# Whitening kernel: every matmul moved into 64x64 tiles of the array, with centring on GpSimd and stores from SyncE

## The reference

```python
mean = x1.mean(-1, keepdims=True)
xc = x1 - mean
cov = xc @ xc.transpose(0, 2, 1) / M + EPS * jnp.eye(G, dtype=x.dtype)
decorr = isqrt_newton_schulz(cov, N_ITER)
y = weight1 @ decorr @ xc + bias1
```

## Time and profile before

| what | value |
|---|---|
| median of 3 runs | 510.39 us |
| the three runs | 490.27, 510.39, 511.94 us |
| span of the profiled execution | 506.6 us |
| median less the span | 3.8 us |
| instructions in the span | 17928 |
| read from and written to HBM | 75.51 MB and 75.50 MB |
| mean rate of the DMA engines | 300 GB/s |
| TensorE busy, by matmuls | 450.2 us |
| TensorE busy, by weight loads | 285.0 us |
| VectorE busy | 329.5 us |
| ScalarE busy | 342.5 us |
| GpSimd busy | 56.6 us |

### The profile page before, as it was taken

One profiled execution on the slowest core, in us unless ns is written; L12 is line 12 of the kernel. 1 busy time (PEld: TensorE's weight loads), 2 busy tenths in 40 slices (PEclk: granted clock), 3 DMA queues, 4 the chain that ended last, 5 costly groups with the idle time before them and its releaser, 6 DMA issues.

```text
span 506.6 us, 17928 instructions
## 1 busy us (share of the span) xinstructions
PE 450.2 (89%) x7872; PEld 285.0 (56%) x7872; DVE 329.5 (65%) x1043; ACT 342.5 (68%) x450; POOL 56.6 (11%) x108
## 2 busy tenths in 40 slices
PE   3678899999999999999999999999999999888800
PEld 3667766666566666666656666666666556423200
DVE  6886567777877787877777877777777765321000
ACT  5674478887777787877778878888787744433800
POOL 0000001111111111111110111111111111110410
PEclk9795579999999999999999999999999989855855
DMA  8999707999899999999999999999998545635890
GB/s 344 371 420 423 314 3 226 345 361 353 315 340 340 351 337 360 374 380 365 323 363 363 341 376 349 372 340 347 379 361 270 178 153 172 187 119 141 265 285 11
DMA packets 19774, 152.17 MB, mean 300 GB/s; under 512 B 3056, under 2 KB 3056, under 8 KB 3696
## 3 DMA queue, kind: packets, MB, share of 16 engines
q0 software_dynamic: 9952, 75.50, 41.8%
q1 hardware_dynamic: 9744, 75.52, 40.7%
HBM read 75.51 MB, written 75.50 MB: 298 GB/s over the span
## 4 chain that ended last, share of the span: by engine, by line
PE 85%; DMA 2%; ACT 2%; DVE 2%; issue 2%; POOL 1%; SPq 1%; DVEq 0%; POOLq 0%
PE cov_ps L591 32%; PE y_ps L606 32%; PE chain_ps L566 6%; PE chain_ps L562 5%; DMA b_col<-bias 2%; PE shift_ps L525 2%; PE chain_ps L572 2%; ACT image L310 1%; PE chain_ps L541 1%; POOL y L272 1%; PE chain_ps L551 1%; PE chain_ps L574 1%; PE chain_ps L560 1%; PE chain_ps L564 1%; PE chain_ps L558 1%
## 5 line engine op out<-in xcount | busy, mean ns | idle before, releaser
L319 ACT ACTIVATE image<-y_ps,y_bias 128x768 f32<-128x768 f32 x192 | 172.2, 899 | 103.4 <-PE y_ps L606 91.8
L403 DVE STREAM_TRANSPOSE transposed<-image 128x384 f32<-128x384 f32 x384 | 213.5, 571 | 13.0 <-issue 2.0
L591 PE MATMUL cov_ps<-transposed 128*64 128x65 f32 x4608 | 188.4, 235 | 9.6 <-DVE transposed L403 7.3
L606 PE MATMUL y_ps<-image,apply_w 64*64 64x384 f32 x1536 | 180.5, 542 | 1.4 <-ACT image L319 0.9
L591 PEld LDWEIGHTS cov_ps<-transposed 128*64 128x64 f32 x4608 | 161.6, 146 | 18.5 <-issue 11.6
L310 ACT ACTIVATE image<-image,shift 128x1152 f32<-128x1152 f32 x128 | 158.1, 1246 | 1.5 <-DMA image<-x 0.5
L562 PEld LDWEIGHTS chain_ps<-yz 32*32 32x32 f32 x576 | 20.9, 106 | 91.7 <-DVE yz L455 54.2
L270 POOL DMA_DIRECT2D y<-image x34 | 19.4, 570 | 425.9 <-ACT image L319 425.9
L455 DVE COPY yz<-chain_ps 64x64 f32<-64x64 f32 x144 | 29.6, 206 | 45.2 <-PE chain_ps L566 39.2
L606 PEld LDWEIGHTS y_ps<-image,apply_w 64*64 64x64 f32 x1536 | 42.4, 138 | 24.5 <-ACT image L319 9.0
L451 DVE SCALAR_TENSOR_TENSOR t_mat<-chain_ps,eye 64x32 f32<-64x32 f32 x144 | 25.0, 174 | 30.3 <-PE chain_ps L562 28.6
(11 more groups left out here) (61 smaller groups left out, 155.6 us busy)
## 6 DMA issues: line engine op xcount, KB each, us to landing
image<-x SPq DMA_DIRECT2D x63, 1152.0 KB, 10.1
y<-image POOLq DMA_DIRECT2D x31, 1152.0 KB, 9.8
y<-image POOLq DMA_DIRECT2D x62, 576.0 KB, 11.0
image<-x SPq DMA_DIRECT2D x2, 576.0 KB, 4.2
y<-image POOLq DMA_DIRECT2D x3, 384.0 KB, 11.6
y<-image POOLq DMA_DIRECT2D x6, 192.0 KB, 11.3
w_nat<-weight SPq DMA_DIRECT2D x4, 4.0 KB, 10.4
b_col<-bias SPq DMA_DIRECT2D x4, 0.1 KB, 10.7
```

The costliest lines, as they stand in the source:

```text
L319: nc.scalar.activation(xs[slot_of(c, i)][:, :, STRIP * q:STRIP * (q + 1)], y_ps[:, q % 2, :, 0:STRIP], ACT.Identity, bias=y_bias[:, c % 2, ...
L403: nc.vector.transpose(dst, xs[slot_of(c, i)][:, h, of_half:of_half + PIECE // 2]).then_inc(transposed, 1)
L591: ins = nc.tensor.matmul(cov_ps[rows, i, 0:GRAM], xt[q][:, t, 0:WIDE * G], xt[q][:, t, 0:GRAM], start=q == 0 and t < columns, stop=q == IM ...
L606: ins = nc.tensor.matmul(y_ps[out_rows, q % 2, h, 0:STRIP], apply_w[rows, c % 2, i].rearrange("p k g -> p (k g)"), xs[slot_of(c, i)][rows, ...
```

## The change

The kernel was written anew around slots; what it computes is the same.

- **Product on the diagonal.** Row group r multiplies into column group r for both halves, so half 1 is no longer exchanged. Again four matmuls of 384 columns for a slot, two in each of two quarters instead of one in each of four. They are issued as two for half 0 and two for half 1.
- **Covariance on the other two quarters.** A matmul has 64 rows instead of 128 (row group r into column group 1-r) and 66 moving columns. Twice as many are needed: 24 in a slot, 12 in each of the two quarters, issued in two lots of 12.
- **Chain in one 64x64 tile.** The two images of a pair stand in one block-diagonal matrix; a step is one matmul of 64 rows and 64 columns with 32 or 96 moving columns, in the upper left quarter, the one that also has half of the product. VectorE's `factor` and `yz` grow with it (64x64 and 64x96 elements). GATHER no longer uses TensorE: ScalarE copies four 32x33 blocks of an image's covariance, and VectorE adds and finishes them (six operations, one a small transpose). NORM has six operations on VectorE.
- **Waits.** In most steps VectorE goes on to the transpose without waiting for its chain operation to end.
- **Order.** In each half slot TensorE issues a chain step, two product matmuls, then 12 covariance matmuls. The product runs 25 slots behind the covariance (`LAG`), and transposes 4 slots ahead (`LEAD`).
- **Centring** is on GpSimd, in 192 operations of 768 pixels, instead of 128 of 1152 on ScalarE.
- **Stores** are issued by SyncE, two for each image, each with 128 partitions. The load into the slot of image n-1 is issued after the store of image n. The small weights are loaded from ScalarE's queue at the start.

The heart of the diff:

```diff
-                columns = BLOCKS // WIDE
-                places = TILES // WIDE
-                for t in range(places):
-                    rows = slice(WIDE * G * (t % columns), WIDE * G * (t % columns + 1))
-                    ins = nc.tensor.matmul(cov_ps[rows, i, 0:GRAM], xt[q][:, t, 0:WIDE * G], xt[q][:, t, 0:GRAM],
-                                           start=q == 0 and t < columns, stop=q == IMAGE_PIECES - 1 and t >= places - columns)
...
+                for t in range(TILES // 2 * half, TILES // 2 * (half + 1)):
+                    for r in range(2):
+                        tile = xt[q][rows(r), t, :]
+                        ins = nc.tensor.matmul(cov_ps[rows(1 - r), n % 2, 0:WIDE], tile[:, 1:1 + HALF], tile,
+                                               start=q == 0 and t == 0, stop=q == PIECES - 1 and t == TILES - 1)
...
+                for r in range(2):
+                    ins = nc.tensor.matmul(y_ps[rows(r), q % 2, half, 0:STRIP],
+                                           apply_w[rows(r), n // PAIR % 2, n % PAIR].rearrange("p k g -> p (k g)"),
+                                           xs[n % SLOTS][rows(r), half, STRIP * q:STRIP * (q + 1)], start=True, stop=True)
...
+                elif t < FOLD:
+                    a = G if t == FOLD - 1 else 0
+                    ins = nc.tensor.matmul(chain_ps[0:HALF, C_NEXT + a:C_NEXT + 3 * G],
+                                           factor[:].rearrange("p i g -> p (i g)"), yz[:, a:], start=True, stop=True)
...
+            for s in range(TOTAL + LAG):
+                if s == PHASE:
+                    pe.wait_ge(consts_ready, 1)
+                for half in range(2):
+                    for pair, t in chain_steps(s, half):
+                        chain(pair, t)
+                    if 0 <= s - LAG:
+                        output(s - LAG, half)
+                    if s < TOTAL:
+                        covariance(s, half)
...
+            for n in range(IMAGES):
+                pool.wait_ge(shift_copied, n + 1)
+                for q in range(PIECES):
...
+                    part = xs[n % SLOTS][:, h, PIECE * o:PIECE * (o + 1)]
+                    nc.gpsimd.tensor_scalar(part, part, shift[:, n % SHIFT_KEPT:n % SHIFT_KEPT + 1], None,
+                                            ALU.add).then_inc(centred, 1)
...
+            for n in range(IMAGES):
+                sp.wait_ge(y_read, PIECES * (n + 1))
+                for h in range(HALVES):
+                    sp.dma_start(out_v[n, :, h, :], xs[n % SLOTS][:, h, :]).then_inc(stored[n % SLOTS][h], 16)
+                if 1 <= n and n - 1 + SLOTS < IMAGES:
+                    load(n - 1 + SLOTS)
...
+            def covariance_out(n):
+                for r in range(2):
+                    act.wait_ge(cov_done[r], PIECES * (n + 1))
+                i = n % PAIR
+                for b in range(BLOCKS):
+                    a = b % 2
+                    nc.scalar.copy(stats[G * i:G * (i + 1), n // PAIR % 2, b, a:a + RUN],
+                                   cov_ps[G * b:G * (b + 1), n % 2, RUN * a:RUN * (a + 1)]).then_inc(cov_read, 1)
```

More of the change, by code:

```diff
@@ L32 @@
 P = 128
+HALF = 64
 BLOCKS = P // G
@@ L285, in _, with sum_shift @@
         @block.scalar
         def _(act):
-            def sum_shift(r, c, i):
-                n = image(r, c, i)
-                if isinstance(n, int) and n == 0:
+            for b in range(2):
+                act.dma_start(w_nat[G * b:G * (b + 1), :], weight[0]).then_inc(consts_in, 16)
+            for b in range(BLOCKS):
+                act.dma_start(b_col[G * b:G * (b + 1), :], bias[0]).then_inc(consts_in, 16)
+            def sum_shift(n):
+                if n == 0:
                     act.wait_ge(first_in, 16)
@@ new lines, in _ @@
+            sum_shift(0)
+            copy_shift(0)
+            sum_shift(1)
+            for s in range(TOTAL + LAG):
+                pair = s // PHASE - 1
+                if s % PIECES == 0 and 1 <= s // PIECES <= IMAGES:
+                    covariance_out(s // PIECES - 1)
+                if 0 <= pair < PAIRS and s % PHASE == 1:
+                    root(pair)
+                if 0 <= pair < PAIRS and s % PHASE == 2:
+                    half_root(pair)
+                if 0 <= s - LAG:
+                    output(s - LAG)
+                for n in range(1, IMAGES):
+                    if n >= 2 and s == shift_slot(n) - 1:
+                        sum_shift(n)
+                    if s == shift_slot(n):
+                        copy_shift(n)
@@ L373, in _ @@
             for b in range(BLOCKS):
-                rows = slice(G * b, G * (b + 1))
-                then(nc.vector.tensor_copy(eye_col[rows, :], eye[rows, rows]))
-            for b in range(BLOCKS):
-                then(nc.vector.tensor_scalar(shift_mat[:, G * b:G * (b + 1)], eye_col[:],
-                                             -1.0 / (BLOCKS * SHIFT_PIXELS), None, ALU.mult))
-            ahead = [shift_copied, shift_mat_ready] + [cov_read, y_read] * 2 + [cov_done] * IMAGE_PIECES
-            for i, free in enumerate(ahead):
-                nc.vector.memset(credits[:, i:i + 1], 0.0).then_inc(free, 1)
@@ L420, in link, with chain, last @@
+            def chain(pair, t):
+                at = [DVE_TOTAL * pair + dve_before(t)]
+                if t != GATHER:
+                    dve.wait_ge(chain_pe, PE_STEPS * pair + t)
+                def last(ins):
                     at[0] += 1
                     ins.then_inc(chain_dve, 1)
[L422 to L425 removed]
@@ L515, in _ @@
-            phases(dve, phase)
+                    dve.wait_ge(chain_dve, DVE_TOTAL * pair + dve_before(ASIDE + 3))
+                    last(nc.vector.tensor_tensor(RSQ, QUOTIENT, HALF_ROOT, ALU.add))
+            for k in range(2 * LEAD):
+                transpose(k)
+            then(nc.vector.memset(parity[:], 0.0))
+            for b in range(BLOCKS):
+                then(nc.vector.memset(parity[G * b:G * (b + 1), b % 2, :], 1.0))
+            then(nc.vector.tensor_scalar(eps_eye[:], eye_col[0:HALF, :], EPS, None, ALU.mult))
@@ L547, in chain @@
+                for c in range(2):
+                    nc.tensor.matmul(shift_ps[rows(c), 0:1], shift_mat[0:HALF].rearrange("p b g -> p (b g)"),
+                                     shift_sum[0:HALF, n % 2:n % 2 + 1], start=True, stop=True).then_inc(shift_ready, 1)
+            def chain(pair, t):
+                if t == GATHER:
                     return
-                pe.wait_ge(chain_dve, DVE_TOTAL * s + dve_needed(t))
+                done = DVE_TOTAL * pair
+                pe.wait_ge(chain_dve, done + dve_needed(t))
+                z = yz[:, G:3 * G]
@@ new lines, in _ @@
+            pe.wait_ge(shift_mat_ready, 1)
+            shift_of(0)
+            for s in range(TOTAL + LAG):
+                if s == PHASE:
+                    pe.wait_ge(consts_ready, 1)
+                for half in range(2):
+                    for pair, t in chain_steps(s, half):
+                        chain(pair, t)
+                    if 0 <= s - LAG:
+                        output(s - LAG, half)
+                    if s < TOTAL:
+                        covariance(s, half)
+                for n in range(1, IMAGES):
+                    if s == shift_slot(n):
+                        shift_of(n)
```

562 lines of the change are left out of this document (223 added, 339 removed).

## The result

| | before | after |
|---|---|---|
| median of 4 runs each | 507.08 us | 567.81 us |
| lowest and highest | 490.27 to 511.94 | 562.45 to 573.46 |
| ratio, 95% interval | | 1.151 (1.131 to 1.171) |

The change makes the kernel slower by 15%; 432 us and 394 to 480 were forecast. The profiled execution of the changed kernel took 569.98 us, its span 568.2.

A forecast was written before the change was run, and what follows sets the result against it. TensorE's queue was taken to set the end: 77 us to the first product, 4 for early slow slots, 300 for 167 slots, 39 for the last 25 and 8 at the end, a span of 428, so 432 us; range 394 to 480.

The forecast's parts named there:

- Steady slot: 1.63 + 0.17 = 1.80 us: Slots with product and covariance: 1.63 us in TensorE's upper left quarter plus 0.17 for the chain's restart per pair.
- What must keep up: Check of other engines per slot: VectorE 1.6 to 1.7 us, ScalarE 1.15, GpSimd 1.2 a piece, DMA equal to TensorE.
- price each quarter of the array by itself: TensorE, steady part: upper left quarter 1.36 us product plus 0.27 chain, 1.63 a slot; covariance, 1.32, fits beside it.
- the turn of a pair: Chain starting anew every 12 slots: 2 us a pair, 0.17 a slot, with bounds of 0 and 3.3 us a pair.
- I take 1.2, between: GpSimd's centring add of 768 columns: 1.2 us, between 0.74 from a memset and 1.69 from a select.
- rival of another engine: Steady part: VectorE, GpSimd (2.0 us a piece) or DMA takes over, slots of 2.0 to 2.1 us, 472 us; chance 0.10.
- The start: 25 slots without product at 1.2 GHz, 2.7 us each from 9 us on: first product at 77 us.
- full clock at the start: Rival: two dense quarters are granted 2.4 GHz before the product, first product at 50 us, 401 us in all; chance 0.27.
- Rows 5: Earlier trace rows where image 1's L541 starts before image 0's L544, read as quarters running ahead of program order.
- in turn: Rival: matmuls start strictly in program order, so a slot takes 2.94 us and the kernel 623 us; chance 0.05.
- equal footing with TensorE: Loads and stores until image 31 is in: 261 us of DMA against 265 us of TensorE's slots.
- The first four: Cases faster by over 2%: forecast 0.42, full clock at the start 0.27, low clock at the end 0.13, another engine or DMA 0.10.

The follow-up runs named there:

- the run with both bounds lifted: The changed kernel with pieces 1, 3 and 5 of each image centred on ScalarE and every other covariance matmul left out: 432.04 us, ratio 0.869.

## Why the prediction was wrong

The predicted direction was wrong, and the range missed the time by 88 us.

- **"Steady slot: 1.63 + 0.17 = 1.80 us": the step that failed.** The sum takes TensorE's time in the array for the time of a slot. That TensorE must first get its instructions has no term in it, does not stand under "What must keep up", and is no rival either, although their number rises from 15.7 to 23.5 thousand. The term is 1.80 us a slot in the prediction and 2.68 in the trace; 167 x 0.88 = 147 us. Of the difference some 0.6 are stand-stills and 0.2 the low clock behind them. The pricing itself was right: "price each quarter of the array by itself" gave 1.63, and an undisturbed slot takes 1.65; the turn of a pair was put at 0.17 a slot and its waits are 0.16. That the supply is the cause is shown by the ends of the q8 packets 1.2 to 1.6 us ahead of each restart, and by the short stores and the small transfers, which change the time and not TensorE's work. What was to be seen before: 7872 records and as many loads in the earlier trace rows, the q8 line of the page (62 packets for 1.02 MB), and five waits on "issue" before L591 loads with no semaphore, one of them 1.1 us, in a profile whose DMA row is all nines.
- **"I take 1.2, between": GpSimd.** Measured 2.20, outside my bounds of 0.74 and 1.69, which came from a memset and a select with no float32 image to read. The rival of another engine had 2.0 us and 472; the run with half the covariance, where GpSimd is the bound, gave 486. It also set the start of the changed kernel, together with the supply: with half of the centring on ScalarE the first product still came at 69.3 us, with half of the covariance besides at 51.9.
- **The start.** 77 us to the first product were forecast, 71.9 came, for another reason. The clock was to stay at 1.2 GHz with half of the array working. The granted clock is 0.86 in 12 to 60 us, with TensorE busy 32 of 48, and 0.99 in 60 to 72: the clock of the rival "full clock at the start" was granted, though not for its reason. With one-column matmuls among them TensorE was busy for 12.00 of 12 us, and its records were as long as at 1.2 GHz, which that reason does not allow. The rival's time of 50 us did not come, as GpSimd gave a slot only every 2.18 us.
- **The quarters overlap: right.** Rows 5 were read rightly; the rival "in turn" is out. The product at the end takes 1.31 us a slot (32 records in 5.25 us) against 1.36 forecast, and the run with both bounds lifted gives 432.0 us. That this equals the forecast is luck: half of the covariance is left out, its slot of 1.94 is at the limit of DMA and was 1.80 in the sum, and its first product comes at 51.9 us instead of 77.
- **The end: right.** 40 us for the last 25 slots (39 forecast) at a clock of 0.96, and 8.5 us from the start of the last output at 559.72 to the end at 568.2 (8 forecast). The 10 us of nothing are gone.
- **The DMA** was put at equal footing with TensorE: right as far as the run with both bounds lifted goes, 398 GB/s; in the changed kernel it had a share of 0.75 and was the cause in a way not thought of.
- **The chances.** The first four add up to 0.92, and with a tenth of the fourth taken off to 0.91, not 0.89. Two of the signs of being wrong came, slots over 2.1 us and L209 over 1.8. Slower had been given 0.06 in all, nearly all of it for another mechanism.

The Trainium skill ("GPSIMD Engine Reference", 3.1) led to the estimate of 1.15 us for a piece; the trace has 2203 ns, and the measurement decides. And as to the order of matmuls ("TensorE: Matmul & The Clock Gate", Part 3, The mechanism): the start strictly in program order that it states does not hold between quarters (covariance records start at 232.51, ahead of product records at 232.76 that stand before them in the program); across a full-height matmul the starts do wait, as the runs with mixed heights show.

## What to carry to other kernels

Count TensorE's instructions, not only its columns: splitting a matmul into quarters that run side by side kept the array's time (1.65 us a slot against 1.63 worked out) and doubled the loads and matmuls, and here blocks of 256 came every 5 to 6 us beside the image traffic, where TensorE could have used one every 3.5. Take a clean slot of the new profile before blaming the array. When "issue" before an instruction in the middle of a dense row grows, look at the line of the instruction queue, divide the number of instructions by its packets, and count the distances between the gaps. An experiment that is to take work away needs a look at its own trace, whether the work is gone. A unit that is to run in quarters must not hold a matmul of full height between them, and an engine that is given new work needs its duration from a like operation (two-byte or four-byte input, same shape), or the bound kept wide.

## What the runs showed of the hardware that was not expected

- Blocks of 256 instructions (16 KB) come by DMA; before a covariance load TensorE waits for "issue" up to 4.0 us when the data packets are 9216 bytes, 2.7 when they are 2304. Same bytes, same instructions: ratios of 1.146 and 1.011 to the kernel before.
- Some of the stand-stills are followed by a stretch at a granted clock of 0.50, 42.9 us of 300 in the steady part, where the kernel before has none.
- GpSimd adds a column to 128x768 float32 in 2203 ns, 2.87 ns a column, and ScalarE does the same piece in 926.
- A matmul of one moving column instead of 66 saved nothing: one record every 49 ns against every 50.
- Two of VectorE's small operations at the turn of a pair grow beside GpSimd. In the changed kernel:

```profile
L350 DVE TENSOR_SCALAR yz<-cov,col 64x32 f32<-64x32 f32 x16 | 11.2, 699 | 0.6
L351 DVE SCALAR_TENSOR_TENSOR factor<-yz,parity 64x64 f32<-64x64 f32 x16 | 8.8, 550 | 0.6
```

  The last of each, with GpSimd done, take 233 and 216 ns. Of the other 15 of L350, eight end 31 or 32 ns after a piece of GpSimd does, as if they had waited for it; the longest takes 966. The Trainium skill ("SBUF — State Buffer", SBUF: two separate sides) says that a VectorE operation with two inputs or in a fast mode and a GpSimd operation lock each other out of a shared port for a whole instruction; these ends agree with it, and so does the like operation of the kernel before, whose GpSimd does little else than issue stores: L444 there takes 232 ns. No run isolates it.
- Six of twelve tiles at full height among quarter matmuls gave 667 and 669 us, five of twelve in one group a slot 522.
